# Two of six gather passes of a graph kernel become 1024 block products each

## The reference

```python
def _fa_layer(h, row, col, Wt_l, bt_l, Wg_l, bg_l):        # layer L3, twice
    h = h @ Wt_l.T + bt_l
    deg = jnp.clip(jax.ops.segment_sum(ones, row, num_segments=n), 1.0)
    dinv = deg ** (-0.5)
    g = jnp.tanh(h[row] @ Wg_l + bg_l)
    norm = g * dinv[row] * dinv[col]
    out = jax.ops.segment_sum(norm[:, None] * h[row], col, num_segments=n)
    return out + h                                          # then relu
```

## Time and profile before

| | |
|---|---|
| median of 3 runs | 4093.56 us |
| profiled execution | 4094.14 us, span 4092.3 us |
| TensorE, its weight loads | busy 1985.4 us (49%), 1772.0 us (43%) |
| VectorE | busy 1992.6 us (49%) |
| ACT | busy 1125.9 us (28%) |
| GpSimd | busy 2782.3 us (68%), 2908 instructions |
| gathers, L611 | 2496 in all, 0.94 to 0.97 us each |
| moved by DMA | 254.5 MB, mean 62 GB/s |

### The profile page before, as it was taken

The page is one execution under the profiler, slowest core; times in us unless marked ns, Lnnn a source line. Parts: engine busy times, 40 slices in busy tenths (PEclk is TensorE's granted clock), DMA queues, the critical chain, the costliest instruction groups (busy, mean ns, idle before and its releaser), DMA issues.

```text
span 4092.3 us, 47903 instructions
## 1 busy us (share of the span) xinstructions
PE 1985.4 (49%) x11685; PEld 1772.0 (43%) x11686; DVE 1992.6 (49%) x5335; ACT 1125.9 (28%) x3224; POOL 2782.3 (68%) x2908
## 2 busy tenths in 40 slices
PE   5962405666654333466675365555543333433332
PEld 4951304555433333356665354545433333333332
DVE  8989607777743222235555758877721110211111
ACT  4210102233210000057777457777400000000000
POOL 2777777777747777457777267777257777477775
PEclk9985556666666556556556577777756655665565
DMA  2210001121221112233333254444221221311213
GB/s 81 68 34 4 19 23 49 53 53 53 52 46 53 53 53 53 33 90 81 79 79 77 22 149 130 130 131 125 35 56 53 53 53 53 50 53 53 52 53 55
DMA packets 147237, 254.53 MB, mean 62 GB/s; under 512 B 58964, under 2 KB 82931, under 8 KB 146856
## 3 DMA queue, kind: packets, MB, share of 16 engines
q0 software_dynamic: 99328, 193.52, 20.1%
q1 hardware_dynamic: 43354, 47.14, 4.1%
q10 hardware_dynamic: 4430, 12.43, 0.9%
HBM read 236.59 MB, written 16.30 MB: 62 GB/s over the span
## 4 chain that ended last, share of the span: by engine, by line
POOL 61%; issue 23%; PE 6%; DVE 6%; DMA 2%; ACT 1%; DVEq 0%; POOLq 0%; ACTq 0%; SPq 0%
POOL pool L611 28%; POOL arena L611 18%; POOL ACC L611 10%; POOL rec_dram L588 6%; PE psum L1092 2%; PE psum L1130 1%; DVE ACC L2020 1%; ACT pool L712 1%; PE psum L967 1%; DVE pool L1489 1%; PE psum L1120 1%; PE psum L1105 0%; DMA tab_dram<-arena 0%; DMA arena<-tab_dram,tblk 0%; DVE pool L2008 0%
## 5 line engine op out<-in xcount | busy, mean ns | idle before, releaser
L611 POOL DMA_INDIRECT arena<-tab_dram,tblk x832 | 795.2, 956 | 402.2 <-issue 250.7
L611 POOL DMA_INDIRECT pool<-tab_dram,tblk x816 | 774.5, 949 | 420.2 <-issue 247.8
L1260 PE MATMUL psum<-pool 128*128 128x128 f32 x1344 | 313.7, 427 | 556.6 <-DMA pool<-tab_dram,tblk 551.6
L1260 PEld LDWEIGHTS psum<-pool 128*128 128x128 f32 x1344 | 291.1, 329 | 580.3 <-issue 580.3
L588 POOL DMA_INDIRECT rec_dram<-arena,ACC x400 | 393.8, 984 | 195.7 <-issue 119.2
L611 POOL DMA_INDIRECT ACC<-tab_dram,tblk x432 | 407.6, 944 | 131.6 <-issue 131.6
L611 POOL DMA_INDIRECT pool<-tab_dram,arena x416 | 401.4, 965 | 131.4 <-issue 126.4
L1315 PE MATMUL psum<-pool 128*128 128x136 f32 (+1 forms) x1664 | 364.0, 400 | 77.1 <-DVE pool L1944 70.8
L1315 PEld LDWEIGHTS psum<-pool 128*128 128x128 f32 x1664 | 337.1, 291 | 89.4 <-issue 52.1
L1237 PE MATMUL psum<-pool 128*128 128x128 f32 x832 | 192.5, 425 | 313.1 <-DMA pool<-tab_dram,arena 218.2
L1237 PEld LDWEIGHTS psum<-pool 128*128 128x128 f32 x832 | 179.7, 328 | 317.4 <-issue 139.0
(11 more groups left out here) (326 smaller groups left out, 4428.2 us busy)
## 6 DMA issues: line engine op xcount, KB each, us to landing
pool<-dst_dram SPq DMA_DIRECT2D x104, 256.0 KB, 3.5
arena<-tab_dram,tblk POOLq DMA_INDIRECT x832
pool<-tab_dram,tblk POOLq DMA_INDIRECT x816, 2.5
HN<-in_edge_attr_dram ACTq DMA_DIRECT2D x23, 500.0 KB
ACC<-tab_dram,tblk POOLq DMA_INDIRECT x432, 2.5
pool<-tab_dram,arena POOLq DMA_INDIRECT x416
rec_dram<-arena,ACC POOLq DMA_INDIRECT x400, 2.1
tab_dram<-arena SPq DMA_DIRECT2D x24, 256.0 KB
```

The source lines that it names most:

```text
L611: nc.gpsimd.indirect_dma_start(to[:, j, :], None, tab_dram[k], bass.IndirectOffsetOnAxis(ap=idx[:, G * g + j:G * g + j + 1], axis=0)).then ...
L1260: last = nc.tensor.matmul(psum[:, bass.ds(vals[j] * P, P)], row if k in FLIPPED else one, one if k in FLIPPED else row, start=False, stop= ...
```

## The change

Passes 4 and 5 no longer gather. Since their sums have no weight for each edge, what a tile adds from one block of sources is a 128x128 matrix of counts (how many edges of the tile go from this source place to that target place) times the block of the table. There are at most 1024 pairs of a tile and a source block that occurs in it, the items. The counts are the same in both passes.

The list of the items (tile, block of the sources, block of the targets) is worked out by VectorE and TensorE before pass 0 and put into three small DRAM tensors. In pass 1 four steps make tables of the edges' source and target places for each item (`item_fields`, `item_tiles`, `turn_fields`, `pick_ends`, in groups 2, 5 and 6), and from group 9 on three packs of 8 items are made beside each group of 8 tiles: VectorE makes two one-hot matrices for each item, one operation for eight (`item_onehots`), TensorE multiplies them, four products into bank 7 at a time (`pack_items`), ACT copies the four counts to SBUF as bf16 (`item_counts`), and SyncE stores each pack of 256 KB in `items_dram` (33.5 MB in all). Bank 7 is no longer free for the row 0..127, so the one-hots of pass 1 read it in SBUF, by an operation with two SBUF inputs.

In passes 4 and 5 SyncE loads the counts again, 16 items at a time, VectorE casts them to f32, 8 at a time (a bite), and TensorE multiplies each with the block of the table in SBUF and adds it to the PSUM slice of the target's block. Two register values address a product, that of the table and that of the slice; 16 are loaded for a bite. The tables of these passes are not stored. The sums of pass 4 now come out node by node; they are scaled by VectorE (`next_sums`) and turned by TensorE (`turn_sums`), and `spread_degrees(1)` is gone. The diff's core, without indentation common to a part:

```diff
+ITEMS = 1024
+PACK = 8
+PACKS = ITEMS // PACK
+PACKS_A_GROUP = 3
+FIRST_PACK = 9
+BITE = 8
+BITES = ITEMS // BITE
-PASSES = ["sum", "sum", "part", "part", "sum", "sum"]
+PASSES = ["sum", "sum", "part", "part", "block", "block"]
...
+items_dram = nc.dram_tensor("items_dram", (P, ITEMS * P), BF16).ap()
+tile_dram = nc.dram_tensor("tile_dram", (1, ITEMS), F32).ap()
+behind_dram = nc.dram_tensor("behind_dram", (1, ITEMS), BF16).ap()
+where_dram = nc.dram_tensor("where_dram", (1, 2 * ITEMS), I32).ap()
...
@@ SyncE
    if k == 1:
+        for b in range(PACKS):
+            sp.wait_ge(s_itemc, C_PICKS + 2 * (b + 1))
+            sp.dma_start(items_dram[:, PACK * P * b:PACK * P * (b + 1)], packed[b % PACKS_A_GROUP]).then_inc(s_kept_items[b % PACKS_A_GROUP], 16)
...
+for k in (4, 5):
+    for n in range(0, BITES, 2):
+        if k == 5 or n >= LONG:
+            sp.wait_ge(s_cast, BITES * (k - 4) + n + 2 - LONG)
+        at = n % LONG * BITE * P // 2
+        sp.dma_start(pool2[:, at:at + BITE * P].bitcast(BF16), items_dram[:, BITE * P * n:BITE * P * (n + 2)]).then_inc(s_bite[n // 2 % 4], 16)
...
@@ GpSimd
-for k in range(len(PASSES)):
+for k in range(4):
...
@@ ScalarE, item_counts()
+    def keep(b, slot, i, peeled):
+        for part in range(2):
+            act.wait_ge(s_itemp, P_PICKS + 2 * b + part + 1)
+            if part == 0 and not peeled:
+                act.wait_ge(s_kept_items[slot], 16 * i)
+            nc.scalar.activation(packed[slot][:, 512 * part:512 * (part + 1)], bank[7][:, :], ACT.Copy).then_inc(s_itemc, 1)
...
@@ TensorE
+def pack_items(b, slot):
+    pe.wait_ge(s_itemv, V_TILES + 2 * b + 2)
+    for part in range(2):
+        pe.wait_ge(s_itemc, C_PICKS + 2 * b + part)
+        for j in range(4):
+            lo, hi = P * (4 * part + j), P * (4 * part + j + 1)
+            last = nc.tensor.matmul(bank[7][:, P * j:P * (j + 1)], onehots[slot][0][:, lo:hi], onehots[slot][1][:, lo:hi],
+                                    start=True, stop=True)
+        last.then_inc(s_itemp, 1)
...
+def turn_sums(c, n):
+    pe.wait_ge(s_weighted, before(7, c, SUMS) + 1)
+    if c >= 2:
+        pe.wait_ge(s_nodes, c - 1)
+    for q in range(n):
+        last = nc.tensor.transpose(bank[(7, 0)[c % 2]][:, q * P:(q + 1) * P], acc3[:, 4 * c + q, 0:D], ident[:, :])
+    last.then_inc(s_itemp, 1)
...
+def item_regs(n):
+    _, vals = nc.values_load_multi_w_load_instructions(
+        where[0:1, bass.ds(2 * BITE * n, 2 * BITE)], engines=[pe.engine], min_val=0, max_val=NB - 1,
+        skip_runtime_bounds_check_because="the table holds block numbers of at most NB - 1")
+    return vals
+def block_pass(k):
+    table = big[:, 2 * NP:2 * NP + NB * AW]
+    clear_sums(k)
+    pe.wait_ge(s_itemrow, ROWS_THERE + 48)
+    pe.wait_ge(s_table, CHUNKS * k)
+    for n, slot, i in bites(pe):
+        vals = item_regs(n)
+        pe.wait_ge(s_cast, BITES * (k - 4) + n + 1)
+        for j in range(BITE):
+            item = bite32[slot % 4][:, P * j:P * (j + 1)]
+            of = table[:, bass.ds(vals[j] * AW, D)]
+            last = nc.tensor.matmul(psum[:, bass.ds(vals[BITE + j] * P, P)], item, of,
+                                    start=False, stop=False)
+        last.then_inc(s_part, 1)
+    close_sums().then_inc(s_part, 1)
...
@@ TensorE, end
-spread_degrees(1)
 flow((0, turn(5)), (1, make(5, wT[:, 4, :])), (2, back(5)))
 flow((0, turn(6)), (1, make(6, wT[:, 5, :])), (2, side(6, ZT, cols[:, 12:13], 1)), (2, back(6)))
-sum_pass(4)
-flow((0, make(7, wT[:, 6, :])), (1, side(7, ZT, cols[:, 13:14], 1)), (1, back(7)))
-sum_pass(5)
+block_pass(4)
+flow((0, turn_sums), (1, make(7, wT[:, 6, :])), (2, side(7, ZT, cols[:, 13:14], 1)), (2, back(7)))
+block_pass(5)
...
@@ VectorE
+def item_onehots(b, slot):
+    dve.wait_ge(s_itemp, P_PICKS + 2 * (b - 3) + 2)
+    for e in range(2):
+        v.tensor_tensor(onehots[slot][e].rearrange("p (w n a) -> p w n a", w=PACK, a=2),
+                        iotab.rearrange("p (n a) -> p n a", a=2).unsqueeze(1).to_broadcast([P, PACK, P // 2, 2]),
+                        ends[e][:, bass.ds(PACK * b, PACK), :].unsqueeze(2).to_broadcast([P, PACK, P // 2, 2]),
+                        ALU.is_equal).then_inc(s_itemv, 1)
...
@@ VectorE, long_pass()
-            v.tensor_tensor(OH8[slot], numbers.unsqueeze(1).to_broadcast([P, G, P]),
...
+            v.scalar_tensor_tensor(OH8[slot][:, j, :], iota[:, 0:P], one[:, R_DST:R_DST + 1], one[:, R_W:R_W + 1].to_broadcast([P, P]),
+                                   ALU.is_equal, ALU.mult).then_inc(s_ohw, 1)
...
+                item_onehots(b, at)
+    dve.wait_ge(s_dst, 32)
+    for b in range(PACKS_A_GROUP):
+        dve.wait_ge(s_kept_items[b], 16 * ((PACKS - 1 - b) // PACKS_A_GROUP + 1))
     dve.wait_ge(s_part, parts + GROUPS)
...
@@ VectorE, block_pass()
+    for n, slot, i in bites(dve):
+        dve.wait_ge(s_bite[slot // 2], bite_loads(k, i))
+        if k == 5 or there(n - 4):
+            dve.wait_ge(s_part, parts + n - 3 if there(n - 4) else parts + n - 4)
+        v.tensor_copy(bite32[slot % 4], bite16[slot]).then_inc(s_cast, 1)
+    dve.wait_ge(s_part, parts + BITES + 1)
...
@@ VectorE, between passes 4 and 5
+def next_sums(c, n):
+    v.tensor_tensor(acc3[:, 4 * c:4 * c + n, 0:D], sums_of(4, c, n), dinv_out[:, 4 * c:4 * c + n].unsqueeze(2).to_broadcast([P, n, D]),
+                    ALU.mult).then_inc(s_weighted, 1)
 def next_nodes(c, n):
-    to = feature_chunk(FT, c, n)
-    v.tensor_tensor(to, sums_of(4, c, n), feature_chunk(HT, c, n), ALU.mult).then_inc(s_weighted, 1)
-    dve.wait_ge(s_weighted, before(7, c, SUMS) + 1)
-    v.tensor_tensor(to, to, feature_chunk(ZT, c, n), ALU.add).then_inc(s_nodes, 1)
-
-dve.wait_ge(s_spreadc, 2 * CHUNKS)
-flow((0, next_nodes), (4, gated_table(7)))
-sum_pass(5, False)
+    dve.wait_ge(s_itemp, P_PICKS + 2 * PACKS + c + 1)
+    v.tensor_tensor(feature_chunk(FT, c, n), bank[(7, 0)[c % 2]][:, 0:n * P].rearrange("p (b f) -> p b f", b=n),
+                    feature_chunk(ZT, c, n), ALU.add).then_inc(s_nodes, 1)
+flow((0, next_sums), (3, next_nodes), (7, gated_table(7)))
+block_pass(5)
```

326 lines of the change are left out of this document (260 added, 66 removed).

## The result

The changed kernel takes 3957.12 us (median of 4 runs, 3956.02 to 3958.04) where the kernel before takes 4094.73 on the same chips (4 runs): a ratio of 0.966, 95% interval 0.9649 to 0.9672. The forecast was 3597 us, range 3530 to 3715. The sign is right; 138 us are gained and not 497. The profiled execution has a span of 3954.7 us. All times are of runs at the chips' usual speed, but for the first four experiments, whose chip was slower outside the block passes (the kernel before took 5308.85 us there), so that they are read by pass 4 alone, and one run of wide (7852.8 us) is left out.

What follows compares the result with a forecast made beforehand. Gathers were taken to bound passes 4 and 5, TensorE's sequencer their replacement. From 4094.1 us: 536.3 less for these passes, 3 more between them, 34 in pass 1, 2 before pass 0, giving 3597; range 3530 to 3715.

Steps and rivals of the forecast that it cites:

- The sign: Whole kernel: the change makes it faster, 4094.1 to 3597 us; chance of faster 0.97.
- the third of passes 4 and 5: Passes 4 and 5: TensorE's sequencer bounds a bite, one load plus eight products, taken as 2.05 us, 266.4 a pass.
- its upper bound 2.46: Passes 4 and 5: slowest bite if each register load takes the longest a load took, 1.112 us.
- What bounded the kernel before: Passes 4 and 5: gathers one behind another, 1.246 us each, 1069.1 us for both passes, 26% of the span.
- Array, cast, loads: Passes 4 and 5: array 1.71 a bite, cast some 0.7, loads 128 GB/s at 2.05 a bite; the sequencer bounds instead.
- The clock: Block passes: TensorE granted 0.9 or more, after the earlier profile's stretch 60:260 with clock 0.98 at 181 of 200 us busy.
- the first rival: Block passes: upper clock not granted, 3.42 us a bite, 442 a pass, 3948 us in all; chance 5%.
- Between the passes: Between passes 4 and 5: 25 transposes and one more VectorE round added, 3 us more (0 to 8).
- Before pass 0: Before pass 0: some 60 small VectorE operations hidden under GpSimd's scatters, 2 us more, of 0 to 6.
- Pass 1: Pass 1: groups of 10.5 us set by TensorE's and ACT's turns in bank 7; 34 us more, 9 to 75.
- the row 2400:2850: Earlier profile: 358 gathers in 450 us beside VectorE busy 347, taken to show gathers there wait only for their buffers.
- my bound of 1.4: Pass 1: upper bound in us for one VectorE item operation, two 512-element operations of 0.70; 11.2 a group.

Runs made afterwards that it cites:

- the first four experiments: no_cast, fixed_blocks, load_kept and one_value: edits of passes 4 and 5 of the changed kernel, one run each; 5128.73, 4734.68, 4736.83 and 4774.84 us on the slower chip.
- wide: scaled with the register values of two bites loaded at once, 32 for 16 products, and one wait for both casts; 3688.85 us, ratio 0.8998.
- scaled: Changed kernel with block numbers turned into element offsets before pass 0, one register instruction a product, still 16 values a bite; 3730.52 us, ratio 0.9097.
- one_word: Changed kernel with both offsets of a product in one 32-bit value, parted by mask and division, 8 values a bite; 3855.32 us.
- word: wide with both places of a product in one value, parted without a mask by one fused instruction, 16 values for two bites; 3638.66 us, ratio 0.888.
- one_value: Changed kernel loading only the 8 table block numbers a bite, product j adding to fixed PSUM slice j; 4774.84 us on the slower chip, 2.00 a bite.
- load_kept: Changed kernel still loading 16 values a bite, but only the first product uses two, seven have constant addresses; 4736.83 us on the slower chip, 1.81 a bite.
- fixed_blocks: Changed kernel with constant addresses for all products of passes 4 and 5 and no block numbers loaded; 4734.68 us on the slower chip, 1.80 a bite.
- word_skew: word with TensorE's chunks between passes 4 and 5 shifted by one, so a chunk's next product comes a step later; 3632.54 us, ratio 0.8867.
- short_turns: Changed kernel with pass 1's bank 7 turns cut to one bf16 product and a 128-column copy, from the fourth pack on; 3952.97 us, ratio 0.964.
- no_item_onehots: Changed kernel with VectorE's two one-hot operations of a pack in pass 1 cut to 8-column copies, from the fourth pack on; 3955.64 us.
- both_short: Changed kernel with the cuts of short_turns and no_item_onehots together in pass 1, from the fourth pack on; 3936.07 us, ratio 0.9609.
- onehot_scalar: Changed kernel with pass 1's weighted one-hots made by an operation with one SBUF tensor input and edge values as scalars; 3950.65 us, ratio 0.9636.
- no_cast: Changed kernel with each bite's cast cut from 1024 columns to 8, but for a pass's first eight bites; 5128.73 us on the slower chip, pass 4 435.4 us.

## Why the prediction was wrong

**The step that failed is the third of passes 4 and 5, TensorE's sequencer, "A bite is 0.59 and 8 x 0.156, 1.84", its value 2.05 and its upper bound 2.46.** All versions fit one account of the sequencer, in us: a bite costs the load, 0.235 around each load, for each register instruction its own length and 0.062 behind it, and 0.22 for the rest. The 0.062 is scaled against the changed kernel: 0.90 less for 8 instructions fewer and 8 x (0.106 - 0.055) of length. The 0.235 comes out of wide against scaled: 0.16 less, of which the loads are 1.107 - 2.131/2 = 0.04, so half of it is 0.12. The 0.22 is what scaled leaves. So changed, scaled and wide give the three constants; one_word, word and one_value test them. In load_kept the account and the array's own time are the same, so that row tests nothing.

| kernel | load a bite | register instructions of a product | account | measured |
|---|---|---|---|---|
| changed | 1.105 | 0.074 + 0.032 | 3.40 | 3.40 |
| one_word | 0.591 | 0.032 + 0.084 | 2.97 | 2.98 |
| scaled | 1.107 | 0.055 | 2.50 | 2.50 |
| wide | 2.131 for two | 0.055 | 2.34 | 2.34 |
| word | 1.106 for two | 0.094 | 2.14 | 2.14 |
| one_value | 0.590 | 0.055 | 1.98 | 2.00 |
| load_kept | 1.105 | one product of eight | 1.79 | 1.81, the array's 1.80 |

Against that account my sum had three errors in one row. The load of 16 values was taken at the length of 8, plus 0.11 for all that I did not know: 0.59 for 1.105. The addition was priced at its own 0.032, without the 0.06 that follows every register instruction; the old beat of 0.124 held that gap once, and I added none for the second. And the fused operation grew from 0.046 to 0.074. (The Trainium skill, Perfetto Trace Analysis, Sequencer-only Instruction, says that the profile shows only the execution of such an instruction, and its decoding and the push behind it come on top; the trace agrees, and puts the price at 0.06.) A product costs 0.245 and not 0.156, eight of them 0.71, the load 0.51, the rest 0.13: 1.35 a bite, 345 us in 256. The upper bound took the longest load on record, 1.112, near the right number by chance (all loads of that line are of 8 values), but left the products at 0.156; a bound on a sum needs a bound on each term.

**Point by point.** What bounded the kernel before was read rightly: the gathers are gone and nothing else of them came back. *Array, cast, loads*: none of them binds; fixed_blocks runs at the array's 1.80 (1.71 forecast) with 145 GB/s. *The clock*: 1.00, as expected from 60:260, although TensorE is busy for only 65%; the first rival is out. Its 3.42 a bite and 3948 us lie beside the measured 3.40 and 3957, but by coincidence: the products run at the upper clock and the array stands still in between. *Between the passes*: 8.4 us more and not 3, since a turn stands in TensorE's queue behind the chain of the chunk before (word_skew); I had counted the work added and not its place in the queue. *Before pass 0*: 2 forecast, 1.9 measured (the first gather starts at 606.9 where it started at 604.9).

**Pass 1**: 44 us longer, 34 forecast, inside 9 to 75; its mechanism is half right. Rows of the changed kernel in the middle of the pass: an item operation of VectorE (two in 1.29), turns of TensorE and ACT, a gather of 1.31, and two groups' f32 products:

```profile
1504.81 1.29 DVE L2060 TENSOR_TENSOR arena<-fwd,arena 128x1024 bf16<-128x1024 bf16 x2 [0.98 <-PE psum L1420]
...
1505.30 0.61 PE L1420 MATMUL psum<-arena 128*128 128x128 bf16 x4 [0.69 <-ACT pool L882]
1505.60 1.31 POOL L710 DMA_INDIRECT ACC<-tab_dram,tblk  x1 [0.30 <-issue]
...
1506.60 0.61 PE L1420 MATMUL psum<-arena 128*128 128x128 bf16 x4 [0.69 <-ACT pool L882]
1507.68 3.69 PE L1444 MATMUL psum<-arena,ACC 128*128 128x128 f32 x16 [0.47 <-issue]
...
1518.21 3.55 PE L1444 MATMUL psum<-arena,ACC 128*128 128x128 f32 x16 [0.47 <-issue]
```

A turn is 1.30 (1505.30 to 1506.60) at the lower clock, forecast 1.38, and groups are 10.5 apart (1507.68 to 1518.21), forecast 10.5. But the gathers did not keep their 1.246 beneath: 400 / 305 is 1.31, because a gather beside a VectorE operation with two SBUF inputs takes 1.00 to 1.03 us on the mean and not 0.944 (counted over 1300 to 1700), as the one of 1.31 at 1505.60 does beside the pair from 1504.81. I had priced that at nothing, at most 10 us; it is 0.065 on a gather, 22 us over the 43 groups, and shows little only since TensorE's beat lies on it (short_turns, no_item_onehots, both_short). The Trainium skill (SBUF — State Buffer, Who interferes with whom) states that such operations contend with a GpSimd instruction that reads SBUF; this trace agrees, and the row 2400:2850 that I set against the rule was of passes whose VectorE work I had not sorted by its inputs. The Trainium skill (VectorE: DVE Perf Modes, The perf-mode tier table) gave an estimated 0.6 for an item operation; the trace agrees, 0.65 (1.29 for two), and my bound of 1.4 from the nearest row was more than twice too high.

By place, the 44 us are 24 in the 43 groups with packs, 6 in the nine groups before them and 14 between the last gather and the next pass (80.4 us where 66.6 were). Of the 24, 3.5 are in the two stretched gathers where the packs begin. Of the 6, for which I had 2 and another reason, the three stretched gathers of groups 0, 2 and 5 are the whole (6.5 us, onehot_scalar): the same contention, at its worst where VectorE's operations follow one another without a pause. Of the 14, where I had 9, both_short takes away 6 (74.0 us); the rest is open. That the 44 lie inside 9 to 75 owes much to the width of the range.

The ledger against the forecast: block passes 345 us more, between them 5, pass 1 10, all else within 1; together 360 us, the whole miss.

## What to carry to other kernels

Where an engine's instructions are addressed by registers, write its sequencer's account first: values loaded, register instructions for each use with the gap behind each, and compare the sum with the array's time; put ready offsets in the table, and let one load serve many uses. The releaser named ahead of an engine's idle time is the last event and need not be the cause (here it was not, no_cast): when the two engines "alternate" although buffers are deep, look at the sequencer's rows in the gap. When a cut frees nothing, look for a second beat of the same length before giving up the cause, and cut both. Sort VectorE's work beside gathers by the number of its SBUF inputs, and look at the longest gathers and not only at the median: the median was 0.94 to 0.95 in every version, and single ones took up to 5.22.

## What the runs showed of the hardware that I had not expected

- A load of values into TensorE's registers takes 0.59, 1.105 and 2.13 us for 8, 16 and 32 values.
- It cost nothing where the array had enough handed over: 1.81 a bite with a load of 1.105 in it (load_kept), against 1.80 without (fixed_blocks).
- A register instruction holds the sequencer for about 0.06 us beyond its own length; a fused one takes 0.046 (the kernel before), 0.055 (scaled) or 0.074 (the changed kernel), and 0.084 to 0.094 with a division among its steps (one_word, word).
- TensorE kept a clock of 1.00 at 65% busy in the block passes, while pass 1 had 0.63 at 62% (248 of 400).
- A gather that started 0.13 us ahead of 16 VectorE one-hots with two SBUF inputs each, one after another, took 5.22 us, until after the last of them; with one SBUF tensor as input of the one-hots, none of the gathers beside them took over 1.06.
- An address may be let run out of 32 bits on purpose: word multiplies by 512 a value with the target's number from bit 23 up, and the table's block is found.
